# First query half's softmax sums: added up by GpSimd in a slot of the ring, with a new slot table and order table

## What is computed

```python
qkv = jnp.clip(jnp.einsum('bsd,ed->bse', xn, Wqkv), -8, 8)
q, k, v = jnp.split(qkv, [D_MODEL, 2 * D_MODEL], axis=-1)
q = _layer_norm(q, q_ln_w, q_ln_b); k = _layer_norm(k, k_ln_w, k_ln_b)
scores = jnp.einsum('bqhd,bkhd->bhqk', q, k) * scale + slopes * rel
probs = jax.nn.softmax(jnp.where(causal, scores, -1e30), axis=-1)
out = jnp.einsum('bhqk,bkhd->bqhd', probs, v).reshape(B, S, D_MODEL)
x = x + out @ Wout.T + (xn @ (alpha * sign(W)).T + bias)
```

## Time and profile before

| | us |
|---|---|
| median of 3 runs | 1428.4 |
| lowest and highest | 1427.1, 1435.53 |
| profiled execution | 1435.19 |
| its span | 1433.4 |
| mean granted TensorE clock | 0.98 |

### The profile page before, as it was taken

How to read it: one execution, slowest core, us unless ns; L and a number is a source line. 1 busy time by engine, 2 the same in 40 slices (tenths; PEclk the granted TensorE clock), 3 DMA queues, 4 the chain that set the end, 5 groups by cost and what they waited for, 6 DMA issues and landing times.

```text
span 1433.4 us, 36801 instructions
## 1 busy us (share of the span) xinstructions
PE 1354.4 (94%) x15272; PEld 681.4 (48%) x15272; DVE 755.1 (53%) x1758; ACT 572.3 (40%) x1081; POOL 489.1 (34%) x332
## 2 busy tenths in 40 slices
PE   3899999999999999799999999999999999879998
PEld 2455444454544444344345555555555555434443
DVE  7566255454555541112677777887788778001111
ACT  4444123332232230000056676777777777600000
POOL 5222022222222220000015455554445555645443
PEclk8899999999999999899999999999999999989999
DMA  6444122222222326521112222223232231224543
GB/s 241 155 162 153 74 64 75 66 66 67 66 66 73 81 66 138 165 88 67 60 47 78 78 80 83 78 78 93 85 94 86 83 92 44 92 68 161 151 157 118
DMA packets 142885, 137.46 MB, mean 96 GB/s; under 512 B 81184, under 2 KB 109984, under 8 KB 142560
## 3 DMA queue, kind: packets, MB, share of 16 engines
q1 hardware_dynamic: 45725, 90.63, 19.6%
q10 hardware_dynamic: 97027, 44.89, 12.2%
HBM read 92.90 MB, written 42.21 MB: 94 GB/s over the span
## 4 chain that ended last, share of the span: by engine, by line
PE 72%; issue 10%; DMA 7%; DVE 5%; POOL 4%; SPq 1%; ACT 1%; POOLq 0%; ACTq 0%; DVEq 0%
PE ps L986 43%; PE ps L1061 7%; PE ps L1122 7%; PE ps L1145 6%; PE ps L1150 5%; DMA arena<-arena 5%; DVE ps L891 2%; PE ps L1039 2%; PE ps L1125 1%; PE ps L1155 1%; POOL small L526 1%; SPq L352 1%; DMA v_scr<-arena 1%; POOL small L522 1%; DMA arena<-in_k_fill 1%
## 5 line engine op out<-in xcount | busy, mean ns | idle before, releaser
L986 PE MATMUL ps<-arena 128*128 128x512 f16 x3584 | 797.6, 383 | 29.3 <-DVE arena L860 10.4
L986 PEld LDWEIGHTS ps<-arena 128*128 128x128 f16 (+1 forms) x3584 | 348.8, 99 | 451.5 <-issue 22.8
L717 ACT ACTIVATE arena<-ps 128x512 f32<-128x512 f32 (+3 forms) x768 | 338.0, 498 | 155.3 <-PE ps L1125 105.3
L584 POOL TENSOR_TENSOR arena<-arena 128x2048 f32<-128x2048 f32 (+1 forms) x48 | 201.7, 4202 | 385.0 <-ACT arena L717 382.5
L891 DVE CUSTOM_DVE_ANT_0 ps<-ps,arena 128x128 f32<-128x128 f32 (+3 forms) x512 | 239.4, 518 | 60.4 <-PE ps L1061 58.2
L1122 PE MATMUL ps<-arena 128*32 128x512 f16 (+3 forms) x3072 | 255.8, 328 | 4.0 <-ACT arena L717 2.5
L1061 PE MATMUL ps<-arena 127*32 127x512 f16 (+3 forms) x3072 | 238.2, 329 | 16.6 <-DVE arena L891 15.4
L860 DVE TENSOR_SCALAR arena<-ps 128x1024 f32<-128x1024 f32 x48 | 58.8, 1225 | 253.6 <-PE ps L986 225.7
L895 DVE TENSOR_REDUCE arena<-ps 128x1 f16<-128x512 f32 x256 | 162.8, 682 | 15.7 <-PE ps L1061 15.7
L1145 PE MATMUL ps<-arena 128*32 128x512 f32 (+3 forms) x1536 | 162.2, 489 | 1.1 <-DMA arena<-v_scr 0.6
L1122 PEld LDWEIGHTS ps<-arena 128*32 128x32 f16 x3072 | 95.4, 96 | 78.4 <-ACT arena L717 29.2
(11 more groups left out here) (51 smaller groups left out, 844.3 us busy)
## 6 DMA issues: line engine op xcount, KB each, us to landing
arena<-in_x SPq DMA_DIRECT2D x32, 512.0 KB, 4.9
arena<-in_wqkv_t SPq DMA_DIRECT2D x48, 256.0 KB, 4.0
base_scr<-arena SPq DMA_DIRECT2D x16, 512.0 KB, 2.8
q_scr<-arena ACTq DMA_DIRECT2D x16, 512.0 KB, 4.1
k_scr<-arena ACTq DMA_DIRECT2D x16, 512.0 KB, 4.5
v_scr<-arena SPq DMA_DIRECT2D x16, 512.0 KB, 2.9
arena<-r_scr SPq DMA_DIRECT2D x32, 256.0 KB
arena<-base_scr SPq DMA_DIRECT2D x16, 512.0 KB, 4.2
```

Source lines behind the costliest of these rows:

```text
L584: nc.gpsimd.tensor_tensor(acc[:, :, at:HALF], former, p32[k % PSLOTS][:, :, 0:w], ALU.add)\
L717: nc.scalar.activation(p32[k % PSLOTS][:, j, 0:w], ps[:, TRB[x % RB], 0:w], ACT.Exp, scale=SCALE).then_inc(exp_done, 1)
L986: ins = nc.tensor.matmul(dst[c], lhs(k, a), wparts[:, k, b, c * HALF:(c + 1) * HALF], start=(k == 0 and (a, b) == order[0]), stop=(k == KT ...
```

## The change

GpSimd now sums half 0: it adds chunks 1, 2 and 3 into the slot of chunk 0, in place (`add_first`), after the value product of chunk 0. The four ones products of half 0 become one of 512 columns over that slot, at the end of chunk 3's turn, which waits for the three adds. Slots are dealt by a table (SLOT, with column offsets: chunks 2 and 3, and 10 and 11, share one), and HELD names for each chunk the chunk whose use must be over before the exponential may write there. NATS and PV_AFTER are new. SyncE sends row A before the reciprocals of the former half, VectorE takes the reciprocals at items 18 and 31 instead of 22 and 32, and ScalarE's copies and casts move by a head or a chunk.

```diff
--- before.py
+++ after.py
@@ -244,6 +244,7 @@
         st_done = sem("st_done")
         exp_done = sem("exp_done")
         add_done = sem("add_done")
+        add0_done = sem("add0_done")
         pv_done = sem("pv_done")
         o_out = sem("o_out")
         s_out = sem("s_out")
@@ -285,12 +286,12 @@
             at = max(0, P * t - HALF * qb)
             return qb, t, at, HALF - at
 
-        NATS = [3, 4, 3, 4, 2, 5, 3, 4, 5, 3, 3, 3]
+        NATS = [3, 4, 2, 4, 3, 4, 4, 4, 5, 3, 3, 3]
         assert sum(NATS) == ITEMS
 
 
-        PV_AFTER = {(0, 2): [-2], (2, 1): [-1], (3, 0): [0], (4, 2): [1], (5, 2): [2], (6, 2): [3],
-                    (7, 1): [4], (8, 2): [5], (9, 1): [6], (10, 0): [7], (11, 0): [8], (11, 2): [9]}
+        PV_AFTER = {(0, 2): [-2], (2, 2): [-1], (3, 0): [0], (4, 0): [1], (4, 3): [2], (5, 2): [3],
+                    (6, 1): [4], (7, 1): [5], (8, 2): [6], (9, 0): [7], (10, 2): [8], (11, 1): [9]}
 
         def due(c, j):
 
@@ -299,13 +300,31 @@
 
 
         ADDED = (1, 2, 3, 5)
-        DIRECT = [qb == 0 or t not in ADDED for qb, t in CHUNKS]
+        DIRECT = [qb == 1 and t not in ADDED for qb, t in CHUNKS]
         ADDS = len(ADDED) - 1
+        ADDS0 = QT // 2 - 1
+        FIRST_ADDS = {4: [1], 5: [2, 3]}
+
+
+
+        SLOT = [(0, 0), (1, 0), (2, 0), (2, 2 * P), (3, 0), (1, 0), (2, 0), (0, 0), (3, 0), (1, 0), (2, 0), (2, 2 * P)]
+
+
+        HELD = [-5, -3, -2, -1, -4, 1, 3, 3, 4, 5, 6, 6]
+
+        def slot(c):
+            i, col = SLOT[c]
+            return p32[i][:, :, col:col + span(c)[3]]
 
         def adds_for(k):
 
             n, c = k // NC, k % NC
-            return 0 if DIRECT[c] else ADDS * n + max(1, ADDED.index(CHUNKS[c][1]))
+            return ADDS * n + max(1, ADDED.index(CHUNKS[c][1])) if CHUNKS[c] in [(1, t) for t in ADDED] else 0
+
+        def adds0_for(k):
+
+            n, c = k // NC, k % NC
+            return ADDS0 * n + c if 0 < c <= ADDS0 else 0
 
         V_FIRST = NT - 4
 
@@ -480,9 +499,10 @@
                 row_b_in(n)
                 if n > 0:
                     sums_out(blk_no(n - 1, 1))
-                    recips_in(blk_no(n - 1, 1))
                 if n < GROUPS - 1:
                     row_a_in(n + 1)
+                if n > 0:
+                    recips_in(blk_no(n - 1, 1))
                 sums_out(blk_no(n, 0))
                 recips_in(blk_no(n, 0))
 
@@ -580,18 +600,29 @@
                 if t == ADDED[1]:
                     need(pool, pv_done, n * NC)
                 need(pool, add_done, adds_for(k) - 1)
-                former = p32[(k - 1) % PSLOTS] if t == ADDED[1] else acc[:, :, at:HALF]
-                nc.gpsimd.tensor_tensor(acc[:, :, at:HALF], former, p32[k % PSLOTS][:, :, 0:w], ALU.add)\
-                  .then_inc(add_done, 1)
+                former = slot(c - 1) if t == ADDED[1] else acc[:, :, at:HALF]
+                nc.gpsimd.tensor_tensor(acc[:, :, at:HALF], former, slot(c), ALU.add).then_inc(add_done, 1)
+
+            def add_first(n, c):
+
+                at = span(c)[2]
+                k = n * NC + c
+                pool.wait_ge(exp_done, GH * (k + 1))
+                pool.wait_ge(pv_done, n * NC + 1)
+                need(pool, add0_done, adds0_for(k) - 1)
+                total = slot(0)[:, :, at:HALF]
+                nc.gpsimd.tensor_tensor(total, total, slot(c), ALU.add).then_inc(add0_done, 1)
 
             for n in range(GROUPS):
                 for c in range(NC):
-                    if not DIRECT[c] and CHUNKS[c][1] > ADDED[0]:
+                    if CHUNKS[c] in [(1, t) for t in ADDED[1:]]:
                         add_in(n, c)
+                    for first in FIRST_ADDS.get(c, []):
+                        add_first(n, first)
                     if n > 0:
-                        if c == 1:
+                        if c == 0:
                             o_norm(n - 1, 0)
-                        if c == 4:
+                        if c == 2:
                             o_low(n - 1, 0)
                         if c == 7:
                             o_norm(n - 1, 1)
@@ -711,10 +742,12 @@
                 x = GH * k + j
                 w = span(c)[3]
                 if j == 0:
-                    need(act, pv_done, k - PSLOTS + 1)
-                    need(act, add_done, adds_for(k - PSLOTS))
+                    former = n * NC + HELD[c]
+                    need(act, pv_done, former + 1)
+                    need(act, add_done, adds_for(former))
+                    need(act, add0_done, adds0_for(former))
                 act.wait_ge(st_done, x + 1)
-                nc.scalar.activation(p32[k % PSLOTS][:, j, 0:w], ps[:, TRB[x % RB], 0:w],
+                nc.scalar.activation(slot(c)[:, j, :], ps[:, TRB[x % RB], 0:w],
                                      ACT.Exp, scale=SCALE).then_inc(exp_done, 1)
 
             def os_copy(n, qb):
@@ -742,11 +775,11 @@
                     for j in range(GH):
                         exps(n, c, j)
                         if n > 0:
-                            if (c, j) == (2, 0):
+                            if (c, j) == (2, 1):
                                 o_high(n - 1, 0)
-                            if (c, j) == (2, 1):
+                            if (c, j) == (2, 2):
                                 os_copy(n - 1, 1)
-                            if (c, j) == (10, 3):
+                            if (c, j) == (11, 3):
                                 o_high(n - 1, 1)
                             if (c, j) == (2, 3) and n < GROUPS - 1:
                                 if n == 1:
@@ -755,7 +788,7 @@
                                 load_vg(act, n + 1)
                             if j == 3 and 3 <= c < 3 + LOADS and n + 2 < GROUPS:
                                 load_part(act, n + 2, c - 3)
-                        if (c, j) == (6, 2):
+                        if (c, j) == (5, 2):
                             os_copy(n, 0)
             o_high(GROUPS - 1, 0)
             os_copy(GROUPS - 1, 1)
@@ -940,9 +973,9 @@
                         nat_item(n + 1, pos)
                     elif pos == 0:
                         row_out(n, use(GROUPS, 0), row_b, rowb_ld)
-                    if pos == 22 and n > 0:
+                    if pos == 18 and n > 0:
                         recips(n - 1, 1)
-                    if pos == 32:
+                    if pos == 31:
                         recips(n, 0)
 
             def c_out_step(t, p):
@@ -1131,7 +1164,7 @@
                 n, c = k // NC, k % NC
                 qb, t, at, w = span(c)
                 first, last = t == 0, c == QB_END[qb]
-                p, v = p32[k % PSLOTS], vg[n % 2]
+                p, v = slot(c), vg[n % 2]
                 pe.wait_ge(exp_done, GH * (k + 1))
                 if first:
                     need(pe, o_out, blk_no(n, qb))
@@ -1142,13 +1175,17 @@
                     return ps[j * DH:(j + 1) * DH, bank, at:HALF]
 
                 for j in range(GH):
-                    ins = nc.tensor.matmul(dst(O_BANK, j, at), v[:, t, j, :], p[:, j, 0:w], start=first, stop=last)
-                if first:
+                    ins = nc.tensor.matmul(dst(O_BANK, j, at), v[:, t, j, :], p[:, j, :], start=first, stop=last)
+                if DIRECT[c]:
+                    if first:
+                        need(pe, s_out, blk_no(n, qb))
+                    for j in range(GH):
+                        ins = nc.tensor.matmul(dst(S_BANK, j, at), ones_w, p[:, j, :], start=first, stop=False)
+                if last and qb == 0:
                     need(pe, s_out, blk_no(n, qb))
-                if DIRECT[c]:
+                    pe.wait_ge(add0_done, ADDS0 * (n + 1))
                     for j in range(GH):
-                        ins = nc.tensor.matmul(dst(S_BANK, j, at), ones_w, p[:, j, 0:w],
-                                               start=first, stop=last and qb == 0)
+                        ins = nc.tensor.matmul(dst(S_BANK, j, 0), ones_w, slot(0)[:, j, :], start=True, stop=True)
                 if last and qb == 1:
                     pe.wait_ge(add_done, ADDS * (n + 1))
                     for j in range(GH):
```

## The result

The changed kernel takes 1456.9 us (median of 4 runs, 1455.74 to 1460.95), the kernel before 1429.22 us beside it (1427.1 to 1435.53): a ratio of 1.0185, 95% interval 1.0152 to 1.0218. It is slower by 1.9%. The profiled execution took 1456.11 us.

A forecast was written before the change was run, and what follows sets the result against it. TensorE's own matmul stream plus 1.8 us of stalls a group was the bound. Period 31.2 - 1.28 + 2.7 + 0.2 + 0.2 = 33.0; with first and last groups 1438.6, with 12 of clock 1450.5, less luck 1447 us; range 1430 to 1462.

The forecast's parts named there:

- What comes off: Half 0's four ones products on TensorE (2.13 us) become one of 512 columns (0.85): 1.28 us saved a group.
- Where the adds stand: From chunk 0's turn to chunk 3's ones product: GpSimd's chain 7.5 us, TensorE's work 4.8, so 2.7 us stall a group.
- What stall goes: VectorE's waits at line 935 for the first half's sums go with earlier transfers: 1.8 us of stall a group.
- The turn's start and the collision: Chunk 0's values wait 0.2 us for ScalarE's bank copy; VectorE's line 901 meeting a GpSimd add costs 0.2 us.
- the third rival: VectorE's minimum at line 901 waits for a GpSimd add, 1.2 us more in 14 groups, 1464 us; chance 0.08.
- The clock: TensorE's clock falls after the new 2.5 us gap in 7 of 16 groups, 12 us; bounds 0 and 27 us.
- The median: Profiled execution stood 6.8 us above the 1428.4 median; half counted as luck outside what the change removes.

The follow-up runs named there:

- The kernel with the early start: Changed kernel with half 0's sum built in idle slot 3, so GpSimd's adds start some 3.5 us earlier: 1397.55 us, ratio 0.9767.
- the kernel that beats all others: Kernel before with SyncE's new transfer order, reciprocals at item 18 and half 0 summed by GpSimd into idle acc: 1391.99 us, ratio 0.9708.
- the one with its product at (6, 0): Changed kernel with chunk 3's turn at (6, 0) and ScalarE's copies at (5, 3): 1455.39 us; with 28 idle matmuls in its gap 1443.72 us.

## Why the prediction came out as it did

The forecast was slower, 1447 us, with the range 1430 to 1462. The direction, the range and the mechanism of the stall held; the time came out 10 us higher, and the reasoning on the clock was wrong though its sum fits. The 9.9 us are made up of about 6.4 from the period (33.44 at full clock and not 33.0, fourteen times), 1.4 from one long period and 4.2 from the step on the median, less about 2 in the rest, the first and last group above all. By its steps:

*What comes off.* 1.28 us a group were put in. The kernel with the early start takes 30.32 a period, the one with the same tables and TensorE's sums 31.58, so 1.26.

*Where the adds stand.* TensorE's work between chunk 0's turn and the product was put at 4.77 us and is 4.78 (938.12 to 942.90). The chain was put at 7.5 and is 7.95 (938.12 to 946.07): the first add starts 0.37 after TensorE moves on, not 0.25, and each of the two handovers between adds costs 0.17 us, not the 0.06 to nothing that I took from two adds of the output stage. The stall is 3.18 instead of 2.7, and this 0.48 is the term that was mis-sized most, 7 us over the fourteen periods. In the first group the gap is only 1.75 us. That the chain alone sets the product's start is shown by both sides: started earlier it leaves no gap, lengthened it moves the product by the added time.

*What stall goes.* The wait on the sums went, in all fourteen periods. I put a period without it at 31.2 and it is 30.97, which the kernel with the transfers' order alone shows. That kernel is 22.9 us faster than the one before (1407.7 against 1430.55), more than all that the sums on GpSimd could save (1.28 in each of 16 groups, 20 us), and in the changed kernel this part only served to hide nearly half of the loss (ratios of 0.9845 and 1.0185). I had taken it as a saving of 1.8 us a group, and the two periods differ by 32.97 - 30.97 = 2.0. Some of that is clock, which I had overlooked: two of the fourteen periods before had a fall behind the wait on the sums. The gaps, and then the periods:

```profile
789.06 0.62 PE L1061 MATMUL ps<-arena 127*32 127x512 f16 x4 [3.53 <-DVE arena L891]
...
890.47 0.62 PE L1061 MATMUL ps<-arena 127*32 127x512 f16 x4 [2.93 <-DVE arena L891]
```

```profile
763.86:801.36 37.50, 33.97 (x690) 18.70 (x686) 25.72 (x86) 23.75 (x55) 17.34 (x7) 0.91 0.28 75
865.87:901.58 35.71, 32.78 (x691) 18.45 (x687) 25.75 (x86) 23.78 (x55) 17.38 (x7) 0.95 0.28 78
```

TensorE is busy for 33.97 and 32.78 us in these two, and for 31.48 in the period from 933.53, which ran at full clock. That is 3.8 us, 0.27 of the 2.0.

*The turn's start and the collision.* 0.2 us each. The wait for the output bank is 0.29 (937.26 against 936.98 by pitch). VectorE's minimum, which was line 901 and is 934, and the add beside it:

```profile
961.99 3.47 POOL L604 TENSOR_TENSOR arena<-arena 128x1536 f32<-128x1536 f32 x1
965.41 1.17 POOL L593 TENSOR_TENSOR arena<-arena 128x512 f16<-128x512 f32 x1
...
964.54 0.94 DVE L934 TENSOR_TENSOR arena<-arena 128x16 f16<-128x16 f16 x1
```

It starts during the third accumulator add and ends when that add does, as the third rival said: a median of 0.96 us for 16 of them, against 0.43 before, 0.40 with the transfers' order alone and 0.20 in the kernel that beats all others. It comes with the new tables and not with the sums on GpSimd, for it is 0.94 in the kernel with the new tables and TensorE's sums. TensorE loses 0.36 us a little later, at 966.20, where a product waits for VectorE, which has had no pause since; in the last group but one, where it has fewer items to fill the time, 1.74 us (the gap that ends at 1238.53, released by line 934), which is why that period is 34.83 at full clock. Not all of that gap is the add's, since the kernel with the transfers' order has one of 1.03 there. The rival was right in kind, and was worth 0.4 us a group, not the 1.4 of its upper bound. The page "SBUF — State Buffer" of the Trainium skill, section "SBUF: two separate sides", says that a VectorE instruction with two SBUF inputs and a GpSimd one that reads SBUF lock a shared port pair against each other, each for its whole length. The trace agrees: in 15 of the 16 groups line 934 ends 0.02 to 0.04 us after a GpSimd add, and the one that ran with no add beside it took 0.17.

With these, a period at full clock is 30.97 - 1.26 + 3.18 + 0.29 + 0.36 = 33.54, and 33.44 was measured.

*The clock.* 7 falls in 16 groups at 1.7 us were put in, 12 us. There were 8: seven in the fourteen periods, at 1.40 us each (34.84 - 33.44), and one in the last group, behind a gap of 3.56, at 2.1 (39.29 - 37.20), 11.9 together, and the run with idle matmuls gives 11.7 back. The number was right by luck, a smaller price times more falls, and the reason for it was not right. I read it as a question of the gap's length, between 1.81 us that did nothing and 2.47 that did, and passed over the loop's own two gaps that did, 2.93 and 3.53, which are nearer in kind. The experiments contradict that: 2.00 us did it in 10 of 14 periods, 2.59 in 9 and 2.98 in 7. With a steady period the falls come in a nearly steady pattern, one in two at 2.98 us and about two in three at 2.59. So the gap's length alone does not decide; what gives these patterns stays open.

*The median.* I took 3.4 us off for luck in the profiled execution of before. There was none to take off in the changed kernel: its profiled execution (1456.11) is 0.8 under its median. The luck before probably lay in the waits on the sums, which the change removes anyway, so that step took them out twice. No trace of a faster execution of the kernel before shows it; what speaks for it is the spread, 9.2 us over eight executions with these waits and 2.4 over four of the kernel with the transfers' order alone.

## What to carry to other kernels

Work moved to an idle engine is free only if its chain fits between the event that may start it and the instruction that waits for it: compare that length with the bounding engine's own work between the same two points, handovers included, before looking at the engine's average load. A result built in place must wait for the last reader of what it overwrites; another buffer that happens to be idle there can turn a loss of 1.9% into a gain of 2.3%. When a change has several parts, measure them alone, for here two small parts of it were worth 1.5% and were hidden by the rest.

## What was not expected of the hardware

A handover between two dependent GpSimd adds cost 0.17 us (between 1,536 and 1,024 elements, and between 1,024 and 512), where the adds of the output stage showed 0.06. TensorE's clock fell behind gaps of 2.00 us more often (10 of 14 periods) than behind gaps of 2.98 us (7 of 14), and matmuls whose results nobody reads, put into the gap, held it at full speed, for a gain of 11.7 us in the changed kernel and 9 to 12 in the one with its product at (6, 0) (by the ratios and by the medians).
